# Convolutions together, norm behind dt and u, token sum on TensorE and ScalarE, earlier query stacks and negation

## What is computed

```python
# Mamba block on g = _gn(x), per joint over time
xz = g @ W_in.T;  xc, z = split(xz)              # 256 + 256
xc = silu(causal_conv4(xc, conv_w) + conv_b)
dt_in, B, C = split(xc @ W_xproj.T)              # 16, 16, 16
dt = softplus(dt_in @ W_dt + b_dt);  u = dt * xc
h_t = exp(dt_t * A) * h_{t-1} + u_t * B_t;  y_t = sum_s h_t[s] * C_t[s]
y = (y + xc * D_skip) * silu(z)
out = rms_norm(y @ W_out.T) * ln_w + g           # per token
x1 = x + out
# attention, 8 heads of 16
q, k, v = split(ln(x1) @ W)
t = x1 + relu(softmax(q k^T / sqrt(128)) v @ proj_w + proj_b)
# then ln(t), router on its token means, 2 of 8 experts, layer norm, residual
```

## Time and profile before

| | |
|---|---|
| median of 3 runs | 1777.21 us (1776.51 to 1780.95) |
| profiled execution | 1784.96 us, span in the trace 1783.4 us |
| busy | VectorE 1381.3, TensorE 1210.5, ScalarE 1089.9, GpSimd 702.1 us |
| mean granted clock of TensorE | 0.823 |

### The profile page before, as it was taken

One profiled execution on the slowest core, in us unless ns is written; L12 is line 12 of the kernel. 1 busy time (PEld: TensorE's weight loads), 2 busy tenths in 40 slices (PEclk: granted clock), 3 DMA queues, 4 the chain that ended last, 5 costly groups with the idle time before them and its releaser, 6 DMA issues. The chain is left out here.

```text
span 1783.4 us, 21758 instructions
## 1 busy us (share of the span) xinstructions
PE 1210.5 (68%) x7072; PEld 520.4 (29%) x7072; DVE 1381.3 (77%) x2336; ACT 1089.9 (61%) x1993; POOL 702.1 (39%) x399
## 2 busy tenths in 40 slices
PE   5124577867786678667876787578847864884991
PEld 2002231242224222422233223222323222222871
DVE  4798788988898889888988988798879973401575
ACT  3432767676767677667757776677677844663430
POOL 3364235524561356225622553256324640000354
PEclk8555688978898789878996899689968996895996
DMA  2441634145414641363228231814072405003541
GB/s 68 158 138 28 187 56 158 38 168 102 149 47 141 129 146 41 122 158 123 64 69 210 74 113 42 228 57 138 23 193 84 139 10 111 2 1 94 164 128 51
DMA packets 94021, 185.08 MB, mean 104 GB/s; under 512 B 15512, under 2 KB 48564, under 8 KB 93908
## 3 DMA queue, kind: packets, MB, share of 16 engines
q1 hardware_dynamic: 92500, 180.41, 35.0%
q0 software_dynamic: 1408, 3.29, 0.6%
...
## 5 line engine op out<-in xcount | busy, mean ns | idle before, releaser
L1242 DVE TENSOR_TENSOR_SCAN hst<-dA,PS 128x800 f32<-128x800 f32 x256 | 466.2, 1821 | 36.8 <-ACT dA L924 3.6
L975 ACT ACTIVATE probs<-PS 128x400 f32<-128x400 f32 x800 | 343.6, 526 | 119.5 <-PE PS L1542 119.4
L1542 PE MATMUL PS<-q_stack,k_stack 99*128 99x400 bf16 (+1 forms) x896 | 238.4, 358 | 88.7 <-ACT probs L975 41.7
L924 ACT ACTIVATE dA<-dt_rep,a_sb 128x775 f32<-128x775 f32 x256 | 245.6, 962 | 74.4 <-DVE hst L1242 62.9
L1237 DVE TENSOR_TENSOR PS<-u_rep,b_rep 128x800 f32<-128x800 f32 x256 | 267.5, 1045 | 19.0 <-DMA u_rep<-u_dram 6.5
L965 ACT ACTIVATE probs<-PS 128x400 f32<-128x400 f32 x400 | 201.7, 504 | 120.1 <-PE PS L1509 97.5
L1263 DVE CUSTOM_DVE_ANT_0 probs<-PS,probs 128x400 f32<-128x400 f32 x400 | 219.7, 573 | 42.6 <-PE PS L1514 17.2
L1527 PE MATMUL PS<-probs,v_ext 128*32 128x400 f32 (+1 forms) x1792 | 206.1, 538 | 30.7 <-DVE o_raw L1284 24.1
L1508 PE MATMUL PS<-k_stack,q_stack 96*128 96x400 bf16 (+1 forms) x448 | 142.4, 354 | 96.7 <-DVE k_neg L1258 96.7
L794 POOL TENSOR_TENSOR dt_sb<-hst,c_rep 128x800 f32<-128x800 f32 x72 | 135.8, 1886 | 153.5 <-DVE PS L1237 153.5
L727 POOL TENSOR_TENSOR norm_r<-norm_r,neg_half 100x8 f32<-100x8 f32 x24 | 40.8, 1702 | 390.6 <-DVE norm_r L1030 371.9
...
## 6 DMA issues: line engine op xcount, KB each, us to landing
...
```

The costliest lines, as they stand in the source:

```text
L924: nc.scalar.activation(dA[:, i % NDA, :].rearrange("p (j t) -> p j t", t=T)[:, :, 1:T], dt_rep[:, gi, :].rearrange("p (j t) -> p j t", t=T ...
L975: nc.scalar.activation(probs[:, j % NPROB, :], bank(4 + j % 3, HALF), ACT.Exp, scale=ATT_SCALE).then_inc(probs_ready.sem, 1)
L1242: nc.vector.tensor_tensor_scan(hst[:, i % 2, :], dA[:, i % NDA, :], dbu, 0.0, ALU.mult, ALU.add).then_inc(scan_done.sem, 1)
L1542: last = nc.tensor.matmul(bank(4 + j % 3, HALF)[strip], k_stack[:, h, kt * P:kt * P + strip.stop - strip.start], q_stack[:, h, q0:q0 + HAL ...
```

## The change

Maxima stand in steps 7 and 8, units from step 11 on. The first negation stands ahead of step 7's product and scan. In the front, `convolve(1)` follows `convolve(0)`, its projection going to banks 6 and 7; the attention's projection goes to bank 4. `x_project` runs as the halves of xc come, `out_project` in two halves around the projection of dt. dt and u of the first half stand ahead of m's mean square and scaling on VectorE, and the squares behind the logarithm on ScalarE. The token sum is made by two matmuls in PSUM (transposed g plus x times identity), which ScalarE copies to `x_sum`. The variance of the next sample's groups stands behind the first scan and its normalisation behind the second. The stores of the q and k parts have a semaphore each, so that the loads of `q_stack` wait for the first alone.

```diff
@@ -300,7 +300,7 @@
...
         FT_AT = LOW_AT + 4
-        MAX_FROM, MAX_TO = 5, 7
+        MAX_FROM, MAX_TO = 7, 9
         UNIT_FROM, UNIT_TO = MAX_TO + 2, NSTEP - 2
...
@@ -341,7 +341,7 @@
...
         v_copied = sig("v_copied")
-        parts_out = sig("parts_out", 32)
+        parts_out = [sig(f"parts_out{i}", 16) for i in range(2)]
         NSTK = 2 * len(Q_PARTS)
...
@@ -614,18 +614,18 @@
...
                         sp.wait_ge(qk_parts.sem, qk_parts.at(n, i + 1))
-                        sp.dma_start(parts_dram[i], part[:, :, :]).then_inc(parts_out.sem, 16)
+                        sp.dma_start(parts_dram[i], part[:, :, :]).then_inc(parts_out[i].sem, 16)
...
                     for i, (stack, which) in enumerate(((q_stack, Q_PARTS), (k_stack, K_PARTS))):
+                        sp.wait_ge(parts_out[i].sem, parts_out[i].at(n, 16))
                         for r, a in enumerate(which):
...
                 if n is not None:
-                    sp.wait_ge(parts_out.sem, parts_out.at(n, 32))
                     load_stacks(0)
...
@@ -864,25 +864,29 @@
...
                     act.wait_ge(proj_up.sem, proj_up.at(n, 1))
-                    nc.scalar.activation(oT[:, :], wide(6), ACT.Relu, bias=proj_b_sb[:, 0:1]).then_inc(att_ready.sem, 1)
+                    nc.scalar.activation(oT[:, :], wide(4), ACT.Relu, bias=proj_b_sb[:, 0:1]).then_inc(att_ready.sem, 1)
                 if f is not None:
                     silu_x(1)
+                    act.wait_ge(xd_up.sem, xd_up.at(f, 1))
+                    nc.scalar.copy(xd[:, :], wide(2)).then_inc(xd_ready.sem, 1)
+                    absolute(0)
+                    exp_of(f, 0)
+                    ln_of(f, 0)
                 if m is not None:
...
                 if f is not None:
-                    act.wait_ge(xd_up.sem, xd_up.at(f, 1))
-                    nc.scalar.copy(xd[:, :], wide(2)).then_inc(xd_ready.sem, 1)
-                    absolute(0)
-                    exp_of(f, 0)
-                    ln_of(f, 0)
                     silu_z(0)
...
                     nc.scalar.activation(dt_sb[:, 1, :], wide(0), ACT.Relu, bias=b_dt_sb[:, 1:2]).then_inc(dt_relu1.sem, 1)
+                    act.wait_ge(gn_tok_up.sem, gn_tok_up.at(f, 1))
+                    if m is not None:
+                        act.wait_ge(ln1_var.sem, ln1_var.at(m, 1))
+                    nc.scalar.copy(x_sum[:, :, :], tokens(6)).then_inc(xs_ready.sem, 1)
                 if m is None and f is not None:
...
@@ -1097,7 +1101,7 @@
...
                     dve.wait_ge(xz_up.sem, xz_up.at(f, ck + 1))
-                    src = wide(2 * (1 - ck))
+                    src = wide((2, 6)[ck])
                     fthen(nc.vector.tensor_scalar(sp_e[:, ck, :], src, conv_w_sb[:, ck, TAPS - 1:TAPS],
...
@@ -1143,6 +1147,7 @@
...
                     convolve(0)
+                    convolve(1)
                 if m is not None:
...
@@ -1150,14 +1155,17 @@
...
                                             ALU.mult).then_inc(y_ready[1].sem, 1)
-                if f is not None:
-                    convolve(1)
                 if n is not None:
...
                     norm_stats(pthen, norm2, t2, 1e-5).then_inc(ln2_var.sem, 1)
+                if f is not None:
+                    dve.wait_ge(dt_abs.sem, dt_abs.at(f, 1))
+                    nc.vector.tensor_scalar(dt_sb[:, 0, :], wide(2), b_dt_sb[:, 0:1], 0.0, ALU.add, ALU.max).then_inc(dt_relu0.sem, 1)
+                    low_part(0, fthen)
+                    dt_and_u(0)
                 if m is not None:
...
@@ -1168,23 +1176,11 @@
...
                     last.then_inc(normed.sem, 1)
-                if f is not None:
-                    dve.wait_ge(dt_abs.sem, dt_abs.at(f, 1))
-                    nc.vector.tensor_scalar(dt_sb[:, 0, :], wide(2), b_dt_sb[:, 0:1], 0.0, ALU.add, ALU.max).then_inc(dt_relu0.sem, 1)
-                if m is not None:
                     dve.wait_ge(normed.sem, normed.at(m, 1))
                     dve.wait_ge(t2_ready.sem, t2_ready.at(m, 0))
+                    dve.wait_ge(xs_ready.sem, xs_ready.at(m, 1))
                     tthen(nc.vector.tensor_tensor(t1[:, :, :], x_sum[:, :, :], o_rms, ALU.add))
-                if f is not None:
-                    low_part(0, fthen)
-                    dt_and_u(0)
-                if m is not None:
                     norm_stats(tthen, norm1, t1, 1e-5).then_inc(ln1_var.sem, 1)
-                if f is not None:
-
-                    dve.wait_ge(x_in.sem, x_in.at(f, 16))
-                    dve.wait_ge(gn_tok_up.sem, gn_tok_up.at(f, 1))
-                    nc.vector.tensor_tensor(x_sum[:, :, :], x_tok[:, :, :], tokens(6), ALU.add).then_inc(xs_ready.sem, 1)
                 if m is None and f is not None:
...
@@ -1201,7 +1197,6 @@
...
                     group_mean(f + 1)
-                    group_var(f + 1)
                 assert n is None or dve_order_p.count == dve_order_p.per_turn, dve_order_p.count
...
@@ -1221,7 +1216,14 @@
...
+                def negate_keys(half):
+                    dve.wait_ge(stacks_in[half].sem, stacks_in[half].at(n, 16 * NSTK))
+                    nc.vector.tensor_scalar(k_neg[:, 4 * half:4 * half + 4, :], k_stack[0:KST, 4 * half:4 * half + 4, 0:HALF],
+                                            -1.0, None, ALU.mult).then_inc(k_neg_ready.sem, 1)
+
                 for i in range(NSTEP):
+                    if n is not None and i == MAX_FROM:
+                        negate_keys(0)
                     if m is not None:
...
@@ -1245,6 +1247,8 @@
...
                     if f is not None and i == 0:
+                        group_var(f)
+                    if f is not None and i == 1:
                         group_apply(f)
...
@@ -1252,11 +1256,8 @@
...
                             _, _, found = max_item(j)
-                            if j in (0, PER_ACC - 2):
-                                half = min(j, 1)
-                                dve.wait_ge(stacks_in[half].sem, stacks_in[half].at(n, 16 * NSTK))
-                                nc.vector.tensor_scalar(k_neg[:, 4 * half:4 * half + 4, :], k_stack[0:KST, 4 * half:4 * half + 4, 0:HALF],
-                                                        -1.0, None, ALU.mult).then_inc(k_neg_ready.sem, 1)
+                            if j == PER_ACC - 2:
+                                negate_keys(1)
                             dve.wait_ge(relu_ready.sem, relu_ready.at(n, j + 1))
...
@@ -1439,37 +1440,48 @@
...
                     pe.wait_ge(o_tok_ready.sem, o_tok_ready.at(n, 1))
-                    channel_major(o_tok_v, 4).then_inc(oT_up.sem, 1)
-                if n is not None:
-                    pe.wait_ge(oT_ready.sem, oT_ready.at(n, 1))
-                    over_spans(6, proj_w_sb[:, :], oT).then_inc(proj_up.sem, 1)
                 if f is not None:
                     if m is not None:
-                        pe.wait_ge(y_summed.sem, y_summed.at(m, NC_))
-                    project_in(0, 1).then_inc(xz_up.sem, 1)
+                        pe.wait_ge(xs_ready.sem, xs_ready.at(m, 1))
+                    project_in(6, 1).then_inc(xz_up.sem, 1)
+                if n is not None:
+                    channel_major(o_tok_v, 4).then_inc(oT_up.sem, 1)
+                    pe.wait_ge(oT_ready.sem, oT_ready.at(n, 1))
+                    over_spans(4, proj_w_sb[:, :], oT).then_inc(proj_up.sem, 1)
+                if f is not None:
+                    pe.wait_ge(silu_done.sem, silu_done.at(f, 1))
+                    x_project(0)
+                    pe.wait_ge(conv_done.sem, conv_done.at(f, 2))
                 if n is not None:
...
                     last.then_inc(attT_up.sem, 1)
+                if f is not None:
+                    pe.wait_ge(silu_done.sem, silu_done.at(f, 2))
+                    x_project(1).then_inc(xd_up.sem, 1)
                 if m is not None:
...
                         pe.wait_ge(y_ready[ck].sem, y_ready[ck].at(m, 1))
-                    out_project(range(NT)).then_inc(out_up.sem, 1)
+                    out_project(range(NT // 2))
                 if f is not None:
-                    for ck in range(NC_):
-                        pe.wait_ge(silu_done.sem, silu_done.at(f, ck + 1))
-                        last = x_project(ck)
-                    last.then_inc(xd_up.sem, 1)
                     pe.wait_ge(xd_ready.sem, xd_ready.at(f, 1))
                     over_spans(2, w_dt_sb[DT0:P, 0:P], xd[DT0:P, :]).then_inc(dt_up.sem, 1)
+                if m is not None:
+                    out_project(range(NT // 2, NT)).then_inc(out_up.sem, 1)
+                if f is not None:
+                    if m is not None:
+                        pe.wait_ge(y_summed.sem, y_summed.at(m, NC_))
                     project_in(0, 2).then_inc(xz_up.sem, 1)
...
                         pe.wait_ge(t2_ready.sem, t2_ready.at(n, 1))
+                    pe.wait_ge(x_in.sem, x_in.at(f, 16))
                     for k in range(NT):
```

(4 more changed lines are left out.)

## The result

The changed kernel takes **1793.55 us** (median of 4 runs, 1791.03 to 1795.09), the kernel before in the same session 1779.08 (1776.51 to 1781.71): a ratio of 1.008 with a 95% interval of 1.0057 to 1.0103. It is slower by 10 to 18 us. I had forecast 1765, in a range up to 1786. The profiled execution took 1792.27 us, its span is 1790.7; against the trace of before that is 7.3 us more. The medians differ by 14.5. The profiled execution of before lay 5.9 over its median in that session and that of after 1.3 under its own, so what follows are pieces of one trace each, good to a few us in the sum.

What follows compares the result with a forecast made beforehand. VectorE, busy 1381.3 of 1783.4 us, was taken as the bound. Steps -35.4, units -2, fronts +26, prologue +1 and last turn -2 summed to -12.4, from the median 1777.21 to 1765 us; range 1744 to 1786.

Steps and rivals of the forecast that it cites:

- Steps, -35.4 forecast: VectorE's steps: moving maxima two steps later and negation ahead saves 5.06 us a turn, -35.4 in seven turns.
- waits for the stacks (1.66): Step 5: VectorE's wait for the stacks, 1.66 us a turn, goes because it arrives 6.0 us later.
- the first score (2.15): Step 5: the 2.15 us wait for TensorE's first scores goes, covered by step 7's product and scan.
- the three slow intervals: First maxima: 0.42 us idle in each of three intervals goes, 1.25 a turn, since TensorE is already running.
- the 6 us which the prediction priced and set aside: First scores: if TensorE's pause kept the clock at 1.2 GHz, two slow intervals would stay, 6 us worse.
- no longer stands between the two halves of the maxima: Sum over states leaving that place, with two steps' small gaps, gives about 1 us back a turn.
- Units, -2 forecast: Scores, exponentials and products with v beside the steps: -0.3 us a turn, -2 in all; ends -3 and +3.3 a turn.
- Rival 2: Units become the bound, VectorE waiting at copies of o_raw: 3.3 us a turn, +23, hence 1788; chance 0.18.
- Fronts, +26 forecast: Fronts: the chain to the scan ends later, 3.6 us in each of six, about 4.3 in turn 0's.
- upper end of +5: Front: +5 us a front if TensorE, with eight more matmuls and longer idle, falls to 1.2 GHz.
- buys nothing there: Front: the convolution moved up gains nothing, as the second silu waits for the gate, 728.5 against 728.55.
- Prologue +1 and last turn -2: Prologue +1.0 us for ScalarE's copy ahead of the second exponential; last turn -2 as query stacks skip the keys' store.

Runs made afterwards that it cites:

- Experiments 2: Twelve idle matmuls on TensorE between the halves of the maxima: 1782.61 us on the changed kernel, 1749.94 on the kernel before with only maxima and negation moved.
- experiment 6: Kernel before with maxima in steps 9 and 10, units from step 13, negation ahead of step 9: 1847.26 us (1.0369).
- after_warm: Changed kernel plus twelve idle TensorE matmuls between the two halves of the maxima: 1782.61 us (1.0007 of the kernel before).
- the step part: Kernel before with only maxima moved to steps 7 and 8, units from step 11, negation ahead of step 7: 1759.35 us (0.9881).
- experiment 4: Kernel before with one front part each: dt and u ahead, squares behind the logarithm 1808.38 us; convolutions together, with new banks 1807.77; token sum moved 1780.80.
- the two parts' medians: Kernel before with only maxima, units and negation moved, 1759.35 us (0.9881); changed kernel with exactly that undone, 1811.24 us (1.0179).

## Why the prediction was wrong

The direction was wrong mainly through the largest term, the steps: of the 19.7 us between forecast and traces 17.0 are theirs. The failed step is the price of the stretch between the two halves of the maxima, which the sum put at nothing. The runs showed it to cost 17.6 us in the trace of the changed kernel, through TensorE's clock.

- **Steps, -35.4 forecast with -2 for the units; -20.4 measured.** The waits for the stacks (1.66) and for the first score (2.15) went as written: 3.8 a turn, 27 us. A smaller step that failed is the third: "I also let the three slow intervals go, 3 x 0.42". In turn 3 the idle of 0.32 and 0.42 before the third and fourth maximum stayed, so some 0.75 of 1.25 was not gained: 5 us in seven turns. That is nearly the 6 us which the prediction priced and set aside. The reason given, that TensorE "has then been running for 3 us", gains little over before: the first maximum now starts 2.6 us behind the first score (599.98 to 602.61), before 2.0 (595.97 to 597.97).
- **What was missing altogether**, and the largest miss, is the price of the sum over states that left. I wrote that it "no longer stands between the two halves of the maxima" and booked this with the units' gain of "about 1". It was what kept TensorE at work. Without it TensorE stands for 2.13 us, the second half starts at a granted clock of 0.57, and in turn 3 the maxima take 36.09 us in place of 34.17. Experiments 2 and 6 give the clock back, with idle matmuls and with real ones; it is worth 2.1 us a turn, 14 in the trace and about 10 in the medians. That alone does not make the changed kernel faster than the one before: `after_warm` is at 1.0007. With the clock kept at both places the steps of turns 1 to 7 take 968.0 us, 43.5 less than before, more than the 37.4 forecast.
- **The clock rule.** The rows show matmuls at half speed from the end of TensorE's gap of 2.13 us, at 622.08, until 628.7. The Trainium skill (TensorE: Matmul & The Clock Gate, The HAM clock gate) says that the throttled clock is the default and that activity releases it. The traces agree: idle matmuls alone took the first 8 us of the second half from 0.79 to 1.00 and the 4 us at the first maxima from 0.50 to 1.00, in turn 3 of the step part. I had applied the rule to the first scores only, not to the place from which the change takes work away.
- **Units, -2 forecast.** Right in sign. VectorE's idle time from the maxima to the last scan fell from 7.63 to 6.06 us in turn 3 and from 52.5 to 42.8 over the seven, 1.4 a turn where I had 0.3. These 8 us more than forecast hide part of the two misses above. Rival 2, with 0.18 the largest, did not happen; the last copy waited 0.23. It would have at two steps more (experiment 6). Its price of 1788 left the forecast's own -2 for the units in; without it the sum is 1790.
- **Fronts, +26 forecast, +29.2 measured.** Turns 1 to 4 lost 3.4 each where I had 3.6, with every wait within 0.2 us; turn 0 lost 4.9 for 4.3. The rest is the clock in turns 5 and 6 (5.0 and 5.7), close to the term's upper end of +5. The size of this term was right, and so was its chain. That the convolution moved up "buys nothing there" held too, since the second silu starts 13.0 us into the front, before 13.1. What it costs there is open, since experiment 4 has it only with another order on TensorE.
- **Prologue +1 and last turn -2, measured -3.6 and +2.1.** Neither can be told from chance. The same prologue gave 59.7, 60.5 and 62.7 where the unchanged one gave 61.6 to 64.5, and the rest took 330.1 to 335.3 us with the earlier query stacks and 328.4 to 334.8 without. In the last turn the negation's wait fell by 0.4 us, not by 2, though the loads of `q_stack` were issued 2.5 us sooner behind the keys' store (0.37 us in place of 2.85). Why so little of it arrived was not settled.
- **The sum.** -12.4 forecast; +7.3 in the traces, +14.5 in the medians. The interval begins at 10 us. The distance between the two is that of the profiled executions, 5.9 over its median before and 1.3 under it after; the product of the two parts' medians, 1.0058, says 10.
